# Top-eight routing in a two-layer kernel: eight-largest and match-replace instructions in place of counted ranks

## What is computed

```python
E, G, TKG, TOPK, SCALE = 32, 8, 4, 8, 2.5
logits = h @ gate_w.T                       # h: 2048 tokens x 128
scores = sigmoid(logits)
sc = scores + gate_bias
grp = sc.reshape(-1, G, E // G)             # 8 groups of 4 experts
group_scores = top_k(grp, 2)[0].sum(-1)
gidx = top_k(group_scores, TKG)[1]          # the 4 best groups
masked = where(in one of those groups, sc, 0)
tki = top_k(masked, TOPK)[1]                # the 8 best experts of a token
tkw = take_along_axis(scores, tki, axis=1)
tkw = tkw / (tkw.sum(-1, keepdims=True) + 1e-20) * SCALE
combine = (one_hot(tki, E) * tkw[..., None]).sum(1)      # tokens x 32
```

## Time and profile before

| | us |
|---|---|
| median of 3 runs | 3750.16 |
| lowest, highest | 3745.32, 3753.55 |
| the profiled execution | 3755.21 |
| its span in the trace | 3753.5 |
| DVE busy, share of the span | 2241.2, 60% |
| PE busy, share of the span | 3066.9, 82% |
| the stage `route`, from its first DMA issue to the first DMA issue of the next stage | 724.32 to 801.72 |

### The profile page before, as it was taken

How to read it: one execution, slowest core, us unless ns; L and a number is a source line. 1 busy time by engine, 2 the same in 40 slices (tenths; PEclk the granted TensorE clock), 3 DMA queues, 4 the chain that set the end, 5 groups by cost and what they waited for, 6 DMA issues and landing times. The chain is left out here.

```text
span 3753.5 us, 73312 instructions
## 1 busy us (share of the span) xinstructions
PE 3066.9 (82%) x23925; PEld 1648.9 (44%) x23925; DVE 2241.2 (60%) x3755; ACT 2086.3 (56%) x3805; POOL 1286.9 (34%) x1223
## 2 busy tenths in 40 slices
PE   2788886249638888836999999999999999999997
PEld 1332332113312232314665565566556556655653
DVE  6888887652347777764555555545555555555553
ACT  1477676012105666624666666666666666666664
POOL 0000000014225556514543453344335334534540
PEclk6588779579858999978999999999999999999998
DMA  5221121124231211123111111111111111111111
GB/s 198 82 84 53 60 72 67 48 52 112 55 43 28 38 35 34 34 64 104 42 45 42 41 52 30 47 39 48 30 48 53 30 42 44 49 31 52 38 35 41
DMA packets 195374, 200.80 MB, mean 53 GB/s; under 512 B 119109, under 2 KB 125909, under 8 KB 190250
## 3 DMA queue, kind: packets, MB, share of 16 engines
q1 hardware_dynamic: 193938, 195.86, 19.1%
q10 hardware_dynamic: 1080, 0.25, 0.0%
HBM read 100.23 MB, written 29.46 MB: 35 GB/s over the span
## 5 line engine op out<-in xcount | busy, mean ns | idle before, releaser
L2427 POOL TENSOR_TENSOR tr_t<-tr_t 128x512 f32<-128x512 f32 x384 | 488.8, 1273 | 707.4 <-DVE tr_t L2271 707.0
L2434 POOL TENSOR_TENSOR tr_nq<-tr_t,tr_rn 128x512 f32<-128x512 f32 x384 | 392.5, 1044 | 393.4 <-ACT tr_rn L2167 393.4
L1638 DVE TENSOR_REDUCE attn_mp<-attn_ps 128x1 f32<-128x512 f32 (+3 forms) x660 | 394.1, 656 | 143.1 <-PE attn_ps L1494 64.1
L2132 ACT ACTIVATE tr_pr<-tr_ps 128x768 f32<-128x768 f32 x264 | 213.9, 810 | 375.6 <-PE tr_ps L1954 375.2
L2270 DVE TENSOR_TENSOR tr_t<-tr_ps,tr_tab 128x512 f32<-128x512 f32 x384 | 263.3, 686 | 245.8 <-ACT tr_sq L2141 245.8
L2280 DVE TENSOR_TENSOR tr_o<-tr_ps,tr_rd 128x384 f32<-128x384 f32 (+1 forms) x264 | 144.0, 545 | 426.8 <-ACT tr_rd L2157 419.0
L1969 PE MATMUL tr_ps<-tr_w,tr_xs 128*128 128x512 f32 x768 | 372.6, 607 | 29.5 <-DVE tr_xs L2298 26.4
L684 DVE TENSOR_REDUCE attn_mcol<-attn_ps 128x1 f32<-128x512 f32 x548 | 357.4, 682 | 49.4 <-PE attn_ps L529 39.4
L1600 ACT ACTIVATE attn_pr<-attn_ps 128x768 f32<-128x768 f32 (+2 forms) x352 | 295.3, 870 | 150.7 <-PE attn_ps L1521 149.8
L668 ACT ACTIVATE attn_pr<-attn_ps 128x512 f32<-128x512 f32 x512 | 272.7, 600 | 88.1 <-DVE attn_ps L706 68.9
L1954 PE MATMUL tr_ps<-tr_qT,tr_kT 64*128 64x96 f32 (+1 forms) x4224 | 301.8, 283 | 0.0
(11 more groups left out here) (260 smaller groups left out, 5082.7 us busy)
## 6 DMA issues: line engine op xcount, KB each, us to landing
tr_v<-tr_va SPq DMA_DIRECT2D x144, 192.0 KB, 2.6
attn_ka<-scratch_kp SPq DMA_DIRECT2D x72, 294.0 KB
tr_v<-tr_va SPq DMA_DIRECT2D x144, 128.0 KB, 2.4
moe_cb<-scratch_combineT SPq DMA_DIRECT2D x32, 512.0 KB
tr_w<-in_w_half SPq DMA_DIRECT2D x12, 1024.0 KB
tr_v<-tr_va SPq DMA_DIRECT2D x48, 256.0 KB, 2.4
scratch_kp<-proj_parts SPq DMA_DIRECT2D x36, 256.0 KB
attn_km<-scratch_kp SPq DMA_DIRECT2D x72, 98.0 KB
```

What stands on the lines that cost most here:

```text
L1638: dve.tensor_reduce(dst, src, AX.X, ALU.max).then_inc(maxed, 1)
L2427: pool.tensor_tensor(t12[:, slot, i, 0, :], t12[:, slot, i, 0, :], t12[:, slot, i, 1, :], ALU.add).then_inc(summed, 1)
L2434: pool.tensor_tensor(nq[:, slot, i, :].rearrange("p (h e) -> p h e", e=DH), t12[:, slot, i, 0, :].rearrange("p (h e) -> p h e", e=DH), rn[ ...
```

## The change

The ranks of the eight groups stay as they are, written out in place. The ranks of the 32 experts are no longer counted. Instead `sc` gets 0.0 added, one `max` instruction per token tile writes the eight largest of its 32 values to `best`, one `match_replace` per token tile copies the 32 values to `left` with each of those eight replaced by -3.0e38, and `pick` is 1 where `left` and `sc` differ. The tile `cmp` shrinks from [128, 16, 32, 32] to [128, 16, 8, 8]. Among the 16 `max` instructions, and among the 16 `match_replace` instructions, only the last is linked.

```diff
-        cmp_ = st.sb("cmp", [P, NT, E_, E_])
+        cmp_ = st.sb("cmp", [P, NT, EG, EG])
+        best, left = st.sb("best", [P, NT, TOP_K]), st.sb("left", [P, NT, E_])
...
-            def rank(vals, K, out):
-
-                for other in range(K):
-                    for lo, hi, op in ((0, other + 1, ALU.is_gt), (other + 1, K, ALU.is_ge)):
-                        if hi > lo:
-                            last = dve.tensor_tensor(cmp_[:, :, lo:hi, other],
-                                                     vals[:, :, other:other + 1].broadcast_to((P, NT, hi - lo)),
-                                                     vals[:, :, lo:hi], op)
-                link(last)
-                link(dve.tensor_reduce(out, cmp_[:, :, 0:K, 0:K], AX.X, ALU.add))
-
-            rank(grp, EG, t8[:])
+            for other in range(EG):
+                for lo, hi, op in ((0, other + 1, ALU.is_gt), (other + 1, EG, ALU.is_ge)):
+                    if hi > lo:
+                        last = dve.tensor_tensor(cmp_[:, :, lo:hi, other],
+                                                 grp[:, :, other:other + 1].broadcast_to((P, NT, hi - lo)),
+                                                 grp[:, :, lo:hi], op)
+            link(last)
+            link(dve.tensor_reduce(t8[:], cmp_[:], AX.X, ALU.add))
             link(dve.tensor_scalar(gsel[:], t8[:], TOP_GROUPS - 0.5, None, ALU.is_lt))
             link(dve.tensor_tensor(v, v, gsel[:].unsqueeze(3).broadcast_to((P, NT, EG, EPG)), ALU.mult))
-            rank(sc, E_, pick[:])
-            link(dve.tensor_scalar(pick[:], pick[:], TOP_K - 0.5, None, ALU.is_lt))
+            link(dve.tensor_scalar(sc[:], sc[:], 0.0, None, ALU.add))
+
+            for n in range(NT):
+                last = dve.max(best[:, n, :], sc[:, n, :])
+            link(last)
+            for n in range(NT):
+                last = dve.match_replace(left[:, n, :], best[:, n, :], sc[:, n, :], -3.0e38)
+            link(last)
+            link(dve.tensor_tensor(pick[:], left[:], sc[:], ALU.not_equal))
             link(dve.tensor_tensor(pick[:], pick[:], score[:], ALU.mult))
```

## The result

| | median, us | lowest to highest | runs |
|---|---|---|---|
| before | 3750.66 | 3745.32 to 3753.55 | 4 |
| changed | 3707.03 | 3702.76 to 3715.16 | 4 |

The ratio of the changed kernel to the one before is 0.9888, 95% interval 0.9867 to 0.9909: 1.1% faster, 34 to 50 us. The forecast was 3711.5 us, range 3703 to 3725.

The account below looks back on a forecast made before the run. DVE's chain in the route stage was taken as the bound: 46.3 us removed, 1.2 + 2.1 + 4.0 + 0.3 = 7.6 added, so 38.7 off the 3750.2 median gives 3711.5 us, range 3703 to 3725.

Parts of the forecast that it names:

- What bounds the stage: Route stage: DVE's chain alone, busy 57.7 of 58.6 us; a microsecond off it is one off the kernel.
- What is removed: DVE in the route stage: 63 compares, one reduce, a 0.43 us instruction and gaps go, together 46.29 us.
- What is added with one answer: DVE's chain: adding 0.0 to `sc`, 0.46 us, and the not-equal, 0.73 us; together 1.19 us.
- The two unknown operations: DVE's chain: 16 max at 0.13, 2.1 us; 16 match_replace at 0.25, 4.0 us; 0.15 per group's link.
- the extra: Allowance above compare cadence: max 0.13 for writing eight results; match_replace 0.25, near 0.20, for waiting on its values.
- the signs that the prediction named: Changed kernel's DVE timeline: added work 7.6 us; max starts 0.13 apart, durations over 0.2; PE's wait about 20.6 us.
- The clock: TensorE's clock at the expert stage's start: its rise may come earlier or later; nothing added, 2 us either way.
- Whole durations: Rival: the new DVE instructions don't overlap, each costs its length and a gap; 33.6 us off, 3716.6 us; chance 0.19.
- Slower: Rival: max and match_replace pass over their input eight times, 1.8 us a call; 12.5 us slower, 3762.7 us; chance 0.02.
- Given back later: Rival: everything behind the route stage, 2955 us, grows by over 1%; about 3748 us; chance 0.02.

Follow-up runs that it names:

- three comparisons: The changed kernel, unaltered, against the kernel before, three times: ratios 0.9888, 0.9893 and 0.9894.
- eight and twelve blocks: Changed kernel with its block of 16 max and 16 match_replace run eight or twelve times in a row: 3740.22 and 3757.11 us, ratios 0.9974 and 1.0019 to before.
- second trace of before: The kernel before, unaltered, executed once more for another trace: 3750.21 us.
- the third of the changed kernel: The changed kernel, unaltered, run a third time: 3708.67 us against 3746.79 for the kernel before, ratio 0.9894.
- the size experiment: Changed kernel plus four linked max and four linked match_replace at each of 8, 64, 128, 256 and 512 elements: 3717.98 us, one execution.
- the contiguous compares: Kernel before, with compares writing results side by side and the reduce reading with the stride: 3754.87 us against 3747.97, ratio 1.0014.
- the kernel with both ways: Changed kernel with the 63 compares and reduce also run, into unread tiles: 3759.77 and 3759.02 us, ratios 1.0024 and 1.0033 to before.
- every call linked: Changed kernel with every max and every match_replace linked, not only the last of each group: 3719.57 us, one execution.

## Why the prediction was right

**What bounds the stage.** Right. DVE's chain shrank by 40.8 us and the kernel by 40.6 on the average of three comparisons; eight and twelve blocks of the new instructions lengthened it by their own timeline price.

**What is removed**, 46.29 us: right. The second trace of before has 46.26 us for the same rows, and the same instructions put back, without the 0.46 us that turn ranks into a mask, took 45.83.

**What is added with one answer**, 0.46 + 0.73: measured 740.75 - 740.28 = 0.47 and 745.79 - 745.07 = 0.72 us.

**The two unknown operations.** Their mechanism was right (they overlap like the compares of the earlier trace rows, one pass each) and their size was put too high. Sixteen max with the link were priced at 2.1 + 0.15 and took 1.62 us; sixteen match_replace at 4.0 + 0.15 and took 2.70. Of the forecast 7.6 us of added work 5.5 were measured. Most of that miss of 2.1 us, 1.3 of it, is the extra put on top of the compare's 0.10 us, 0.03 for a max and 0.05 for a pair: there was none to add. Taking the row's cadence as it stood, 0.10 for a max and 0.20 for a pair, would have given 1.2 + 1.6 + 3.2 + 0.3 = 6.3. The other 0.8 us come from starts still closer than that, 0.094 us for a max and 0.16 for a pair. Two of the signs that the prediction named were therefore missed, starts 0.13 us apart and durations over 0.2. The extra had been argued from eight results written late and from a replace that must have its values first. The rows show neither as a delay: a max lasts 195 ns when every call is linked and 176 when it isn't, but the one of 194 among the 16 is the first, which has a wait in front of it, so the difference goes with the wait and not with the results; and the replace starts 0.07 to 0.08 us behind its value load, just as that load of 0.08 to 0.09 us ends.

**The clock**, priced at 2 us either way, went the bad way by 1.3. The stretch with the experts was 228.4 and 228.2 us in the first two traces of the changed kernel against 227.0 and 226.9. The rows by stretches at the start of that stage show where, first of the kernel before, then of the changed one (the granted clock is the third number from the right):

```profile
804.10:807.50 3.40, 3.40 (x4) 1.49 (x5) 0.00 (x0) 0.00 (x0) 0.00 (x0) 0.51 0.98 222
807.50:810.90 3.40, 3.40 (x9) 1.44 (x8) 1.37 (x2) 1.19 (x2) 0.00 (x0) 1.00 0.38 84
```

```profile
758.80:762.20 3.40, 3.40 (x4) 1.50 (x5) 0.00 (x0) 0.00 (x0) 0.00 (x0) 0.50 0.99 248
762.20:765.60 3.40, 3.40 (x6) 1.39 (x5) 0.69 (x1) 0.65 (x2) 0.00 (x0) 0.60 0.31 67
765.60:769.00 3.40, 3.40 (x9) 1.52 (x8) 0.93 (x2) 1.14 (x2) 0.00 (x0) 1.00 0.00 0
```

PE is busy throughout in both, but at 1.2 GHz for 3.4 us in the one and for about 6 in the other before it is granted 2.4. A mean of 0.60 over the second stretch is 2.7 us more at half the clock, an estimated 1.4 us of work lost, which is the whole difference. It isn't tied to the change: the second trace of before, the third of the changed kernel (227.0 us), the size experiment (226.9) and the twelve blocks (227.1) had the early rise, the contiguous compares (228.3) the late one. Nor is the rise all that makes this stage long: in the first trace of the kernel with both ways the clock was 0.50 for the first 3.4 us and 0.96 in the next, an early rise, and the stage still took 228.3 us.

**The rivals.** *Whole durations* falls: linked, the instructions do cost them, 8.3 us for the 32 calls; unlinked, 4.3. The Trainium skill's rule (VectorE: DVE Perf Modes, "The DRAIN you can't avoid"), that chaining without semaphores gains nothing, holds neither for the compares (0.10 us from start to start, 0.21 long) nor for these two: the waits left out gained 4.0 us. The same section ends its first paragraph with an exception, that a next op which is not held starts earlier, and the rows go by that. *Slower* falls by the sizes. *Given back later* happened only as the clock's 1.3 us.

**What was right by luck.** The two errors of the sum had opposite signs: 2.1 us too much for the new instructions, 1.3 too little for the clock in two of the three traces of the changed kernel. Where the clock did take its part, the second error hid some of the first: the chain alone says 40.8 us off, against 38.7 forecast. Of the 4.5 us between the forecast and the first median, the two errors account for 0.8; the rest is the spread of runs.

**What stays open.** The kernel with both ways was 9.0 and 12.4 us slower than before, 10.7 on average, where its chain explains 5.05 and the stage with the experts, longer by 1.3 and 0.6 us in its two traces, at most 1.3 more. Nor is the start time the cause (twelve blocks: 7.1 measured, 6.7 by the chain). In the traces, the masks-to-stash stretch took 655.1 to 660.9 us in the five executions of kernels with the 63 expert compares (before twice, contiguous, both ways twice; 658.8 on average) and 650.0 to 656.0 in the nine without (653.5). Nearly all of that difference lies in one stage, the attention of layer 1, which took 535.7 us on average in the five and 531.0 in the nine. This split was seen in the traces only afterwards. If it were an effect of the compares, the change should have gained some 5 us more than its chain, and it gained about 1 (40.6, against 40.8 - 1.3). Nor would it set the kernel with both ways apart from the kernel before, which has the same compares. And all five have a tile of 64 KB on each partition for the compares' results, which none of the nine has, so the traces can't tell compares from tile. One execution each can't settle it, and no run here tells what a stage's instructions could do to one that starts 230 us later. The stretch from the stash to the final stage is open as well: it took 2047.1 to 2048.0 us in eleven traces and 2050.5 to 2050.8 in three, the third of the changed kernel, every call linked and twelve blocks.

## What to carry to other kernels

A stage in which one engine works alone between two barriers is the simplest thing to price: what leaves its chain leaves the kernel's time. Averaged over three comparisons, or with ten or more runs, the sum of the rows held to 1 or 2 us (the changed kernel, eight and twelve blocks, the contiguous compares); a comparison of four runs scattered by some 4 us around it and a single execution by 6 to 8, and the kernel with both ways is an exception that stays open. The eight largest of a short row cost one instruction and 0.09 us a tile on DVE, and comparing against the eighth of them is cheaper than marking the eight by match_replace, where equal scores at the edge need no order; counting ranks costs K squared elements per token and loses at K = 8 already (3.85 against 1.54 us). Instructions that don't depend on one another should stand without a wait between them, and their price is then the distance of starts and not the duration.

## What was not expected of the hardware

- Sixteen max over 32 elements fill 1.59 us, so their starts are (1.59 - 0.18)/15 = 0.094 us apart, although each lasts 0.176 and writes eight values.
- A replace needs the values of the load in front of it, and still starts 0.08 us behind it (742.37, 742.45), as the load of 0.09 us ends and without the gap of some 0.03 us that a linked instruction shows. The next load starts 0.09 us after the replace (742.45, 742.54), which itself lasts 0.18.
- A stride of 128 bytes on the read side made a reduce of 16384 elements take 27.51 us instead of 17.22, and on the write side the compares 28.54 instead of 21.51.
